# A CIN tower on one core: turns later in TensorE's order, and layer 0 multiplied as plain float32

## The reference, cut to what matters

```python
h, outs = inputs, []                       # inputs: (512, 40, 32)
for i, (W, bias) in enumerate(params):     # 3 layers, W: (200, fields * 40)
    x = einsum('bhd,bmd->bhmd', h, inputs).reshape(B, -1, D)
    y = relu(einsum('oi,bid->bod', W, x) + bias[None, :, None])
    if i != n_layers - 1:
        h, direct = split(y, 2, axis=1)    # 100 maps go on, 100 go out
    else:
        direct = y
    outs.append(direct)
z = concatenate(outs, axis=1).sum(-1)      # (512, 400)
h = maximum(concatenate([z, dense_ctx]) @ W_top1 + b_top1, 0)
h = maximum(h @ W_top2 + b_top2, 0)
return h @ W_top3
```

## Time and profile before

| | |
|---|---|
| median of 3 runs | 3135.87 us (3124.83 to 3136.49) |
| profiled execution, span | 3134.4 us |
| TensorE busy | 2930.7 us, 94% |
| VectorE busy | 2622.0 us, 84% |
| ScalarE busy | 1454.5 us, 46% |
| GpSimd busy | 717.0 us, 23% |
| matmuls by heads (line 697) | 9088, mean 373 ns |
| matmuls by tails (line 699) | 9088, mean 259 ns |
| loads of x_pairs per block | 3 of 280.0 KB and one of 120.0 KB |
| DMA | 249.87 MB, mean 80 GB/s |

### The profile page before, as it was taken

One profiled execution on the slowest core, in us unless ns is written; L12 is line 12 of the kernel. 1 busy time (PEld: TensorE's weight loads), 2 busy tenths in 40 slices (PEclk: granted clock), 3 DMA queues, 4 the chain that ended last, 5 costly groups with the idle time before them and its releaser, 6 DMA issues.

```text
span 3134.4 us, 53996 instructions
## 1 busy us (share of the span) xinstructions
PE 2930.7 (94%) x19516; PEld 2888.7 (92%) x19516; DVE 2622.0 (84%) x1751; ACT 1454.5 (46%) x1880; POOL 717.0 (23%) x669
## 2 busy tenths in 40 slices
PE   2899999999999999999999999999999999999999
PEld 2899999999999999999999999999999999999996
DVE  4888888888888888898888888888888888988894
ACT  2554444445445444444444444444444444444452
POOL 1122222222222122222222222222221222221110
PEclk8999999999999999999999999999999999999999
DMA  6332232232332332322322322322323323323221
GB/s 149 98 89 73 79 86 71 80 83 68 90 82 68 89 78 72 90 75 73 86 77 76 90 72 76 85 73 79 87 68 83 82 68 90 79 72 89 77 66 22
DMA packets 269272, 249.87 MB, mean 80 GB/s; under 512 B 16987, under 2 KB 267786, under 8 KB 269149
## 3 DMA queue, kind: packets, MB, share of 16 engines
q1 hardware_dynamic: 200376, 196.52, 19.8%
q0 software_dynamic: 59744, 45.90, 10.2%
q10 hardware_dynamic: 9129, 7.13, 0.9%
HBM read 140.44 MB, written 4.20 MB: 46 GB/s over the span
## 4 chain that ended last, share of the span: by engine, by line
issue 58%; PE 19%; POOL 12%; DMA 8%; ACT 2%; SPq 1%; ACTq 0%; POOLq 0%; DVE 0%; DVEq 0%
PE acc L697 12%; POOL gathered L400 6%; PE acc L699 6%; POOL wait_taker L408 5%; DMA acc_copy<-acc_copy 4%; DMA gathered<-in_table,rows_now 3%; ACT acc_copy L480 1%; POOL acc_copy L409 1%; ACT y_relu L485 1%; PE z_ps L714 1%; PE hid_ps L710 1%; DMA x_pairs<-x_rows 0%; PE acc L756 0%; SPq L316 0%; PE hid_ps L779 0%
## 5 line engine op out<-in xcount | busy, mean ns | idle before, releaser
L697 PE MATMUL acc<-weights,heads 126*128 126x400 f32 (+1 forms) x9088 | 2785.6, 373 | 52.7 <-DVE tails L645 52.5
L699 PE MATMUL acc<-weights,tails 126*128 126x200 f32 (+1 forms) x9088 | 2357.8, 259 | 0.0
L697 PEld LDWEIGHTS acc<-weights,heads 126*128 126x128 f32 (+1 forms) x9088 | 1760.8, 194 | 55.5 <-issue 42.0
L699 PEld LDWEIGHTS acc<-weights,tails 126*128 126x128 f32 (+1 forms) x9088 | 1788.2, 197 | 0.0
L645 DVE TENSOR_TENSOR tails<-product,heads 126x1024 fp32r<-126x1024 f32 (+2 forms) x1152 | 1342.4, 1207 | 258.4 <-ACT heads L474 258.3
L474 ACT ACTIVATE heads<-product 126x1024 fp32r<-126x1024 f32 (+2 forms) x1152 | 1168.0, 1042 | 479.3 <-PE acc L699 339.1
L640 DVE TENSOR_TENSOR product<-hid_rep,x_rep 126x2048 f32<-126x2048 f32 x512 | 1172.8, 2291 | 103.8 <-PE acc L699 68.4
L408 POOL TENSOR_TENSOR wait_taker<-wait_taker 1x1 f32<-1x1 f32 x192 | 187.8, 978 | 2262.6 <-ACT acc_copy L480 2218.0
L485 ACT ACTIVATE y_relu<-acc_copy 128x400 f32<-128x400 f32 x192 | 103.3, 538 | 650.0 <-DMA acc_copy<-acc_copy 650.0
L480 ACT ACTIVATE acc_copy<-acc 128x800 f32<-128x800 f32 x192 | 161.3, 840 | 506.9 <-PE acc L699 501.2
L400 POOL DMA_INDIRECT gathered<-in_table,rows_now x150 | 258.1, 1721 | 45.7 <-issue 45.7
(11 more groups left out here) (27 smaller groups left out, 104.2 us busy)
## 6 DMA issues: line engine op xcount, KB each, us to landing
x_rep<-x_rows SPq DMA_DIRECT2D x512, 125.0 KB
hid_rep<-hid SPq DMA_DIRECT2D x512, 125.0 KB
x_pairs<-x_rows SPq DMA_DIRECT2D x192, 280.0 KB
acc_copy<-acc_copy POOLq DMA_DIRECT2D x192, 200.0 KB
x_pairs<-x_rows SPq DMA_DIRECT2D x64, 120.0 KB
raw_weights<-in_w ACTq DMA_DIRECT2D x12, 492.2 KB
gathered<-in_table,rows_now POOLq DMA_INDIRECT x150
x_rows<-gathered POOLq DMA_DIRECT2D x30, 80.0 KB, 3.4
```

The costliest lines, as they stand in the source:

```text
L697: nc.tensor.matmul(acc[:, at.parity, c, 0:2 * LAYER], heads[0:rows, ring % HEADS_RING, k, cols], w, start=(q == 0 and k == 0), stop=False)
L699: last = nc.tensor.matmul(acc[:, at.parity, c, LAYER:2 * LAYER], tails[0:rows, ring % PRODUCT_RING, k, cols], w[:, 0:LAYER], start=False, ...
```

## The change

Two things change together.

- **Layer 0 in plain float32.** `accumulate_whole` multiplies the unsplit products (`product`) by the unsplit weights (`raw_weights`), 200 columns a call. Its group 0 is summed in the first 200 columns of `acc`, group 1 in the second 200, so that copy, add and relu stay as they are. Layer 0 has no heads, no tails and no split weights. `split_group` counts the groups of layers 1 and 2 alone for `heads_made` and `tails_made`; places in the ring of heads go by the group's number in its layer (`q`).
- **Turns later.** In a full step TensorE's order is: l0's two groups, l1's groups 0 and 1, turn of `before`, l1's groups 2 to 4, turn of l0, l1's groups 5 to 7, l2's groups 0 to 3, turn of l1, l2's groups 4 to 7. ScalarE's order follows: `copy_acc` comes after the heads of four groups of the next slot (for layer 2 after two), `relu` and `copy_turned` later, and l0's `copy_turned` after heads 0 and 1 of l2.

```diff
+        def split_group(layer, b):
+
+            if not isinstance(b, int):
+                return b * (2 * GROUPS) + (split_group(layer, 4) - 4 * (2 * GROUPS))
+            return place(layer, b).group - GROUPS0 * (b if layer == 0 else min(b + layer + 1, blocks))
...
             load_weights(EARLY_LOADS)
-            split_heads(*split_after("start"))
...
                 act.wait_ge(products_made, g + 1)
-                above_zero(act, groups_used, g - (HEADS_RING - 1))
+                skipped = GROUPS0 if layer == 1 and q < HEADS_RING and (not isinstance(b, int) or b + 1 < blocks) else 0
+                above_zero(act, groups_used, g - skipped - (HEADS_RING - 1))
...
             def heads_and_results(slot, previous):
 
-                make_heads(*slot, 0)
-                make_heads(*slot, 1)
+                for q in range(4):
+                    make_heads(*slot, q)
                 copy_acc(*previous)
-                make_heads(*slot, 2)
-                make_heads(*slot, 3)
-                relu(*previous)
                 make_heads(*slot, 4)
                 make_heads(*slot, 5)
-                copy_turned(*previous)
+                relu(*previous)
                 make_heads(*slot, 6)
                 make_heads(*slot, 7)
+                copy_turned(*previous)
...
                     copy_acc(*before)
-                    make_heads(*l0, 0)
                     relu(*before)
-                    make_heads(*l0, 1)
                     copy_turned(*before)
...
                 elif l0:
-                    make_heads(*l0, 0)
-                    make_heads(*l0, 1)
                     if odd is None and i == 0:
                         load_weights(split_until[0] + EARLY_LOADS)
...
-                if before:
-                    copy_acc(*before)
                 split_heads(*split_now(0))
                 for q in range(2) if first else ():
                     make_heads(*first, q)
                 if odd is None and i == 1:
                     load_weights(split_until[1] + 1 + EARLY_LOADS)
                 if before:
-                    relu(*before)
-                if l0 and first:
-                    copy_acc(*l0)
+                    copy_acc(*before)
                 split_heads(*split_now(2))
                 for q in range(2, 4) if first else ():
                     make_heads(*first, q)
                 if before:
-                    copy_turned(*before)
+                    relu(*before)
                 if l0 and first:
-                    relu(*l0)
+                    copy_acc(*l0)
                 split_heads(*split_now(4))
                 for q in range(4, 6) if first else ():
                     make_heads(*first, q)
+                if before:
+                    copy_turned(*before)
+                split_heads(*split_now(6))
+                if first:
+                    make_heads(*first, 6)
+                if l0 and first:
+                    relu(*l0)
+                if first:
+                    make_heads(*first, 7)
+                for q in range(2) if second else ():
+                    make_heads(*second, q)
                 if l0 and first:
                     copy_turned(*l0)
...
                 if second:
-                    heads_and_results(second, first)
+                    for q in range(2, 4):
+                        make_heads(*second, q)
+                    copy_acc(*first)
+                    make_heads(*second, 4)
+                    make_heads(*second, 5)
+                    relu(*first)
+                    make_heads(*second, 6)
+                    make_heads(*second, 7)
+                    copy_turned(*first)
...
-                            make_previous_tails(at.group + q, at.ring + q)
-                        previous[0] = (layer, q)
-                        if odd is None and (i == 0 or i == 1 and (layer, q) in ((0, 0), (1, 0))):
+                            make_previous_tails(split, at.ring + q)
+                        if layer > 0:
+                            previous[0] = (layer, q)
+                        if odd is None and i == 1 and (layer, q) == (1, 0):
...
+            def accumulate_whole(at, b, q):
+                ring = (at.ring + q) % RING
+                if q == 0 and isinstance(b, int) and b == 0:
+                    pe.wait_ge(prep_added, 2)
+                if q == 0:
+                    above_zero(pe, acc_copied, at.slot - 1)
+                pe.wait_ge(products_made, at.group + q + 1)
+                tiles = group_tiles(0, q)
+                for k in range(tiles):
+                    w = raw_weights[0:OPERAND_ROWS[0], GROUP * q + k, LAYER:2 * LAYER]
+                    for c in range(CG):
+                        last = nc.tensor.matmul(acc[:, at.parity, c, q * LAYER:(q + 1) * LAYER],
+                                                product[0:OPERAND_ROWS[0], ring % PRODUCT_RING, k, c * 128:(c + 1) * 128], w,
+                                                start=(q == 0 and k == 0), stop=(q == GROUPS0 - 1 and k == tiles - 1))
+                last.then_inc(groups_used, 1)
...
                 if l0 and first:
                     accumulate(*first, 0)
+                    accumulate(*first, 1)
                 if l0 and before:
                     turn(*before)
-                for q in range(1 if l0 else 0, 3) if first else ():
+                for q in (range(2, 5) if l0 else range(4)) if first else ():
                     accumulate(*first, q)
                 if before and not l0:
                     turn(*before)
                 if l0 and first:
                     turn(*l0)
-                for q in range(3, GROUPS) if first else ():
+                for q in range(5 if l0 else 4, GROUPS) if first else ():
                     accumulate(*first, q)
                 if second:
-                    for q in range(3):
+                    for q in range(4):
                         accumulate(*second, q)
                     turn(*first)
-                    for q in range(3, GROUPS):
+                    for q in range(4, GROUPS):
                         accumulate(*second, q)
```

More of the change, by code:

```diff
@@ L218, in split_after @@
             w2 = list(range(split_until[1], split_until[2]))
-            if i == "start":
-                return list(range(split_until[0]))
             if (i, layer) == (0, 0):
@@ L471, in make_heads @@
                 act.wait_ge(products_made, g + 1)
-                above_zero(act, groups_used, g - (HEADS_RING - 1))
+                skipped = GROUPS0 if layer == 1 and q < HEADS_RING and (not isinstance(b, int) or b + 1 < blocks) else 0
+                above_zero(act, groups_used, g - skipped - (HEADS_RING - 1))
                 rows = OPERAND_ROWS[layer]
-                act.activation(heads[0:rows, ring % HEADS_RING, 0:tiles, :], product[0:rows, ring % PRODUCT_RING, 0:tiles, :],
+                act.activation(heads[0:rows, q % HEADS_RING, 0:tiles, :], product[0:rows, ring % PRODUCT_RING, 0:tiles, :],
                                ACT.Copy).then_inc(heads_made, 1)
@@ L640, in make_products, with make_tails, make_previous_tails @@
                 dve.tensor_tensor(out, first, second, ALU.mult).then_inc(products_made, 2)
-            def make_tails(layer, q, g, ring):
+            def make_tails(layer, q, split, ring):
                 tiles, rows = group_tiles(layer, q), OPERAND_ROWS[layer]
-                dve.wait_ge(heads_made, g + 1)
+                dve.wait_ge(heads_made, split + 1)
                 dve.tensor_tensor(tails[0:rows, ring % PRODUCT_RING, 0:tiles, :],
                                   product[0:rows, ring % PRODUCT_RING, 0:tiles, :],
-                                  heads[0:rows, ring % HEADS_RING, 0:tiles, :].bitcast(F32),
+                                  heads[0:rows, q % HEADS_RING, 0:tiles, :].bitcast(F32),
                                   ALU.subtract).then_inc(tails_made, 1)
             previous = [None]
-            def make_previous_tails(g, ring):
+            def make_previous_tails(split, ring):
                 layer, q = previous[0]
                 for n in (2, 1):
-                    make_tails(layer, q + 2 - n, g - n, (ring - n) % RING)
+                    make_tails(layer, q + 2 - n, split - n, (ring - n) % RING)
                 previous[0] = None
@@ L696, in accumulate @@
                         cols = slice(c * 128, (c + 1) * 128)
-                        nc.tensor.matmul(acc[:, at.parity, c, 0:2 * LAYER], heads[0:rows, ring % HEADS_RING, k, cols], w,
+                        nc.tensor.matmul(acc[:, at.parity, c, 0:2 * LAYER], heads[0:rows, q % HEADS_RING, k, cols], w,
                                          start=(q == 0 and k == 0), stop=False)
```

25 lines of the change are left out of this document (11 added, 14 removed).

## The result

The changed kernel takes 3148.2 us (median of 6 runs, 3138.4 to 3162.1) against 3134.6 us before (6 runs, 3124.8 to 3136.5): ratio 1.006, 95% interval 1.0036 to 1.0085. It is a little slower, 0.6%. The forecast was 2959 us; even the upper end of its range, 3060, was too low. The profiled execution took 3149.5 us, 3147.8 of it the span.

The account below looks back on a forecast made before the run. TensorE, 94% busy, its waits and its clock were taken as the bound. From 3134.4 us, -115 (turns), -91 (clock), +41 (plain float32), -14 (start), +2.5 (end), +1.5 (to the median) gave 2959; range 2925 to 3060.

Parts of the forecast that it names:

- (a): Turns one group later on TensorE: layer 1's ready 9.3 us after the accumulator, asked for at 9.4; gain 115 us.
- (b): Granted clock, 0.97 between 110 and 2943 us: its loss comes from the turns' waits and returns; gain 91 us.
- rival D: SyncE's loads, waiting for layer 0's later maps, bring x_rep too late: slower, 3298 us if 7 us late; chance 0.04.
- The last of the cases: Only layer 0's part takes effect; turns still met 2 us early, chain follows the turn's place: 3164 us; chance 0.02.
- Rival C: Accumulator copy misses VectorE's product, so a tail holds GpSimd and the chain is 1.2 us longer: 3065 us; chance 0.10.
- Rival E: The clock's falls do not come from the turns' waits and stay: 3050 us; chance 0.08.
- (c): Layer 0's plain float32 calls on TensorE: 0.34 us each, 4.76 a block against 4.11; cost 41 us.
- Rival B: Layer 0's plain passes are bound by their weight loads, 0.39 us a call (+90 us): 3008 us; chance 0.13.
- (d): VectorE and ScalarE lose layer 0's tails and heads, but neither bounds a step: 0 us.
- (e): Start: step 0's weight loads issued earlier, TensorE's first group needs no tails: -14 us, ends 0 and -22.
- (f): End: last wait for tails needs hid_rep, loaded behind layer 1's turn, now one group later: +2.5 us.
- cases for faster: The forecast (0.63) and Rival B, Rival C and Rival E, at 3008 to 3065 us; faster given as 0.92.

Follow-up runs that it names:

- e3: Changed kernel with layer 0's turn one group earlier on TensorE and its copy ahead of heads 0 and 1 of layer 2: 2994.5 us, 0.955 of before.
- e5: Changed kernel loading only the first of seven shifted tiles of x_pairs (240 KB, not 960), so another output: 2979.8 us, 0.950 of before.
- e11: Changed kernel with only layer 0's copy on ScalarE moved ahead of heads 0 and 1 of layer 2: 3053.1 us, 0.978 of before.
- e4: Changed kernel with layer 1's turn behind five groups of layer 2, not four: 2952.9 us, 0.942 of before.
- e9: Kernel before (layer 0 split) with the changed orders, layer 1's turn behind five groups, layer 0's turn and copy early: 2923.0 us, 0.936 of before.
- e10: Changed kernel (plain float32) with layer 1's turn behind five groups and layer 0's turn and copy early: 2945.4 us, 0.943 of before.
- e7: Kernel before (layer 0 split) with the changed orders and layer 1's turn behind five groups: 2978.5 us, 0.950 of before.
- e8: Changed kernel with layer 1's turn behind five groups and step 0's further weight loads held until the first products are made: 2954.5 us, 0.942 of before.
- e1: Changed kernel with the old orders of TensorE and ScalarE, leaving plain float32 in layer 0 alone: 3113.3 us, 0.994 of before.
- e2: Kernel before, layer 0 still split, with only the changed orders of TensorE and ScalarE: 3100.1 us, 0.988 of before.

## Why the prediction was wrong

**The step that failed is (a), its sentence on the DMA.** The prediction had "The turn is ready 9.3 us after the accumulator and is asked for at 9.4. What is left over is the spread of the DMA". That took layer 1's adding DMA at its 6.3 us from a row in which the loads had a start of 10 us. The chain is 2.4 + 8.3 + 0.6 = 11.3 us now and not 9.3; the wait 1.8 us and not 0.2. So (a) gave 18 us and not 115, and (b), which hung on it, 6 and not 91; between 110 and 2900 us 87 us are missing in both kernels. The material stood in the prediction itself: it had noted that the layer-1 add "runs while the loads of x_rep flow" and that layer 2's takes 3.1 us by itself, and rival D had the loads 7 us later. I followed the loads to who waits for them and not to what is in flight beside them. That the loads are the cause is shown by e3, e5 and e11, which shorten the add by moving or thinning them, and that the add's length was the loss by e4, which covers it. By what they hold it back is open: in the shown turn the engines' mean share was 31.5% and 21.9%, so they were not all busy. The last of the cases, turns still met 2 us early at 3164 us, is nearest to what happened; it had a chance of 0.02 and no mechanism beyond a chain that follows the turn's place. In e4 their lateness does cost VectorE some 2 us a step, within the 3 us I gave it in D (half of the 12.91 is 6.5 us and not the 9 used there).

**Copy and lock, (a): right.** The copy 1 us later cost nothing, and GpSimd was held for the rest of the product (0.47 us for 1.33). The Trainium skill (SBUF — State Buffer, "SBUF: two separate sides") has the two engines take their shared port by an exclusive lock for a whole instruction; both rows agree, each of the adds ending with the product. Rival C did not happen. Layers 2 and 0 did not wait.

**The clock, (b): mechanism right, but it needs the waits gone.** The 91 us stayed as the waits did. e3, e4, e9 and e10 have 1.00 in the middle with waits of 0.6 us or none; with 1.2 us a step (e11) 0.99, with 1.7 to 2.1 from 0.97 to 0.98. Rival E is out: in e4 the falls go with the waits.

**Plain float32, (c): 32 us for 41.** A pass of 200 columns takes 4.614 / 28 = 0.165 us, shorter than the 0.19 us of a weight load's record, so the loads are hidden behind the passes. By the Trainium skill (TensorE: Matmul & The Clock Gate, "LDWEIGHTS") a load of 128 columns takes an estimated 107 ns, which the trace agrees with in so far as a pass of 165 ns hides it. Rival B is out (its +90 is +86 by its own 0.39).

**VectorE and ScalarE, (d): 0 was right here, not always.** e7 against e4 shows layer 0's tails cost once VectorE has to absorb a late load.

**Start and end.** (e) was -14 and is -3 by difference, about 0 by the fourth block's start: the early weight loads delay x_pairs by 8 us (without them, in e8, the first matmul comes at 29.9), which was the upper bound I had named. (f) was +2.5 and is +3.1.

With the 18 us that the turns gave, nothing for the clock and its other terms as they stood, the prediction would have had 3134.4 - 18 + 41 - 14 + 2.5 + 1.5 = 3147. That this is so near 3148 is luck: (c) was 9 us too high and (e) 11 too hopeful. Two numbers of the prediction do not follow from its own: its sum gives a step of 47.5 - 165 / 64 = 44.9 us and not 44.4, and its cases for faster add to 0.94 and not 0.92.

## What to carry to other kernels

When a step is moved, ask of every transfer that it releases not only who waits for it but what will be in flight beside it: here an add of 200 KB that came to lie beside other loads took 2.1 us more, nearly the whole 2.35 us by which the turn had been moved. A wait that is met by moving the consumer should be met with a margin of the producer's spread (one group more, e4, gave 6%), and a small wait in every step can cost clock besides: between 110 and 2900 us, 87 us of clock were missing beside 124 of waits in the kernel before, 27 beside 72 in e11, and 2 beside 38 in e3. Two changes that each gain are to be timed together as well.

## What the runs showed that I had not expected

- The adding DMA of 200 KB takes 3.1 us with no load beside it, 5.6 with 431 KB, 6.2 with 490, 6.8 with 556, 7.1 with 651, 7.7 with 753 and 8.1 to 8.3 with 844 to 864: some 6 ns a KB. The KB are counted over the add's own length, so a longer add counts more, and this is not a price of a KB. In the first 5.5 us after the issue alone, e1 and e5 both have some 430 KB beside them and take 5.6 and 6.8 us. What is in flight matters too: in the first 3 us the add's queue moved about 147 KB (median) in the kernel before, 141 in e3, e9, e10 and e11, 98 in the changed kernel and 26 in e5. With x_rep issued 2 to 4.6 us ahead of the add it was over 140, with x_rep behind it under 105. Why was not tried.
- The granted clock was not lost in proportion to the waits: 1.8 us a step missed 96 us in e2 and 107 in the changed kernel, 1.7 us 68 in e1, 1.2 us 46, 0.6 us 15. The clock rows show why a mean wait says little. In the kernels that wait, nearly every fall to 1.2 GHz between 110 and 2900 us begins at a turn of layer 1 (from 1.5 us ahead of its start to 4 us behind it), and only some turns have one: 41 of 59 before, 44 of 59 in the changed kernel, 24 of 60 in e1, 31 of 59 in e2, 14 of 61 in e11, none in e3 and e4. Over all thirteen kernels, of 89 turns that waited over 2.0 us 79 had a fall, of 218 with 1.25 to 2.0 us 117, and of 486 with less none. One kernel also differs from one execution to the next: e1's ten missed 68 to 107 us. Why e2 and the changed kernel have 31 and 44 at the same mean wait stays open.
- The best version keeps layer 0 split (e9): 2923.0 us, 0.936 of the kernel before.
